# A vision tower on one core: the scan's B product moved from SBUF to PSUM, and each scan step cut into two feature blocks

## The chip, the cores and the metric

The kernel runs on 1 core of a Trainium2 chip. The metric is device time in microseconds (us) of one execution, lower is better; the kernel before is given by the median of three runs.

## What is computed

The reference is a small two-layer vision tower for 32 images, each 38 tokens of 192 features. Cut to what matters here:

```python
h = tokens(x)                                  # patches @ W + b + pos, two class tokens: (32, 38, 192)
h = h + ssm(layernorm(h))                      # first scan
h = h + moe_ffn(layernorm(h))                  # top 2 of 8 experts, 192 -> 768 -> 192, gelu
h = h + mamba_two_ways(layernorm(h))           # down to 96, a forward and a backward scan, up to 192
h = h + mixture(layernorm(h))                  # top 2 of 8 experts, 192 -> 192

# ssm, per token t, feature d and state n (16 states):
state = (delta * state + (1 - delta) * u * b * dt) * exp(a * dt)
y = sum_n(state * c) + u * D
# mamba, once per direction:
h = exp(dt * A) * h + dt * u * B               # B, C: 16 numbers per token
y = sum_n(h * C) + u * D
```

In both layers the recurrence has the form state = decay x state + input x B, per feature and state, along the tokens.

## The kernel before, in words

The images are worked in 4 groups of 8, so a group has T = 304 tokens. Tokens lie along the free dimension, features or states along the 128 partitions. A **scan step** handles QB = 2 feature blocks; a block is 8 features x 16 states = 128 partitions, so one step works on tiles of 128 x 608. 12 steps (QSTEPS) cover the 192 features. What a step does:

- SP fills one of 4 ring slots (SLOTS) by DMA: decay rows into dA and input rows into BB, both broadcast from a scratch tensor rows_d, 304 KB each.
- ACT raises the decay rows to exp (in the first pass this goes into another tile, and POOL multiplies it into dA, `decay_step`, L678).
- DVE multiplies the input rows by the B states, which lie in a PSUM bank: the **B product**, BB <- BB x B, 128 x 608, back into SBUF (`first_b_product` L1243, `b_product` L1273). It is issued one step ahead: step c issues the product of step c+1, then its own scan.
- In the first pass DVE also forms PR = decay x C from PSUM (L1258).
- DVE runs the **scan**, one tensor_tensor_scan of 608 columns from dA and BB, both in SBUF, into ST (`first_step` L1264, `direction_step` L1287).
- POOL multiplies ST by C or PR (L684, L765), and PE sums the 16 states of each feature into the Y bank (all matmuls go through the helper at L1614).

**First pass.** `first_pass` runs three stages side by side, 12 steps each: the scan of group s, the preparation of group p (patches, layer norm, hidden layers of the A, B, C and delta networks in 11 blocks), and the routing of group m. In step 11 PE forms the B states (B1_BANK) and the C states (C1_BANK) of the next group to be scanned: `states(p, 1, ...)` and `states(p, 2, ...)`, and ACT adds a bias to each in PSUM.

**Expert blocks.** 34 blocks of 128 gathered rows, matmul work mostly. Blocks 0 to 4 are put into the last scan steps of the first pass, others stand alone, and the second half goes into the first steps of the second pass.

**Second pass.** For each group `part_a` is 12 steps of the forward scan and `part_b` 12 of the backward scan. Beside the scan of group g, part_a finishes group g-1 (output norm, up-projection, residual) and brings in group g+1; group g-2's expert mixture, begun in the last step of part_b, runs in steps 0 to 4 of part_a as 6 parts on PE (`mixture`). Each part multiplies two expert inputs, gated by POOL (L773), into two banks: features 0 to 127 into Q_BANK and the rest, 64 features, into QR_BANK. In step 5 DVE adds both to the residual (`add_mixture`, Om at L1524, Or at L1525). After the last group the same code runs with nothing beside it.

The order on every engine is written out by hand in these step functions; an engine runs its list in order and waits on semaphores, which count per group. PSUM has 8 banks of 512 columns, and each user has a fixed bank. The layout before (the hidden blocks take banks 5, 6 and the free Y bank in turn):

```python
        Y_BANK = (3, 0)
        MEAN_BANK, ROUTE_BANK = 4, 7
        B1_BANK, C1_BANK = 1, 2
        HIDDEN_BANKS = (5, 6)
        X_BANK, Z_BANK, L_BANK, Q_BANK, QR_BANK = 6, 5, 5, 7, 4
        AFTER_BANK, BW_BANK = Y_BANK, (1, 2)
```

## Time and profile before

| | |
|---|---|
| median of 3 runs | 999.3 us (997.8, 999.3, 1003.47) |
| span of the profiled execution | 1002.8 us; its own run is not marked, and the run nearest to it is the one of 1003.47 us |
| busy over the span | PE 758.7 us (76%), DVE 650.1 (65%), POOL 445.9 (44%), ACT 406.4 (41%) |
| first pass with scans (48 steps) | about 53 to 307 us of the span |
| expert blocks without scans | about 310 to 524 us |
| second pass with scans (96 steps) | about 524 to 928 us |
| last group's end, no scan beside it | about 928 to 1003 us |

How to read it: the span runs from the first to the last instruction of one execution. "Busy" is the time in which an engine executes; the idle time before an instruction is given with the engine and instruction that released it ([0.67 <-ACT ...]). A record's length contains some overlap with the next one, so the spacing of starts is the better price of an instruction in a full queue.

### The profile page before, as it was taken

What the parts mean: (1) busy time and instruction counts of PE and PEld (TensorE: products, weight loads), DVE (VectorE), ACT (ScalarE), POOL (GpSimd) and SP (SyncE); (2) the same over time, 40 slices, a digit from 0 to 9 for tenths busy, and PEclk for the clock granted to TensorE, in tenths of its full rate; (3) what the DMA queues carried; (4) which work ended last, traced back from release to release, by engine and by line L of the source; (5) the groups of instructions that cost most, each with busy time, mean ns of one, the idle gap of its engine ahead of it and who ended that gap; (6) DMA issues with size and microseconds to landing.
All of it is one profiled execution on the core that took longest, in us unless ns stands there. A gap on an engine that the chain in (4) does not pass through costs nothing.

```text
span 1002.8 us, 11291 instructions
## 1 busy us (share of the span) xinstructions
PE 758.7 (76%) x3552; PEld 591.1 (59%) x3552; DVE 650.1 (65%) x993; ACT 406.4 (41%) x880; POOL 445.9 (44%) x311
## 2 busy tenths in 40 slices
PE   7978797775578798889996686768696869766745
PEld 5655565445358697888883455546474646544524
DVE  4187979899965223122127997798788896799320
ACT  2556392571234242324445354626243543442010
POOL 1167656864954113120003644553475427455403
PEclk8979899786769899999996596989697979885957
DMA  9579654553955688888748577756775757586011
GB/s 342 134 254 332 182 157 116 148 129 82 251 164 168 185 248 247 235 258 250 216 148 220 150 193 175 183 154 152 201 183 150 188 143 203 150 196 177 12 28 56
DMA packets 84667, 179.50 MB, mean 179 GB/s; under 512 B 12740, under 2 KB 32832, under 8 KB 83840
## 3 DMA queue, kind: packets, MB, share of 16 engines
q1 hardware_dynamic: 79776, 171.55, 61.5%
q0 software_dynamic: 4832, 7.24, 2.4%
q8 instruction: 28, 0.46, 0.2%
q14 instruction: 31, 0.25, 0.1%
HBM read 158.02 MB, written 20.69 MB: 178 GB/s over the span
## 4 chain that ended last, share of the span: by engine, by line
PE 28%; DVE 19%; issue 7%; DMA 5%; ACT 3%; SPq 3%; POOL 2%; DVEq 0%; POOLq 0%
PE PS L1614 27%; DVE ST L1287 6%; DMA xp<-slots_d 3%; DVE BB L1273 3%; DMA BB<-rows_d 2%; POOL PR L765 2%; DVE p_WV L1343 1%; DVE p_OM L1340 1%; DVE p_TM L1338 1%; ACT L889 1%; DVE q_OM L1340 0%; SPq L536 0%; SPq L549 0%; POOL WX L773 0%; ACT dA L938 0%
## 5 line engine op out<-in xcount | busy, mean ns | idle before, releaser
L1614 PE MATMUL PS<-PR,CM 128*128 128x304 f32 (+1 forms) x672 | 198.3, 440 | 78.7 <-POOL PR L765 64.4
L765 POOL TENSOR_TENSOR PR<-ST,V 128x608 f32<-128x608 f32 x96 | 160.5, 1674 | 190.8 <-DVE ST L1287 166.6
L1614 PEld LDWEIGHTS PS<-PR,CM 128*128 128x128 f32 x672 | 135.2, 235 | 126.8 <-POOL PR L765 82.8
L1287 DVE TENSOR_TENSOR_SCAN ST<-dA,BB 128x608 f32<-128x608 f32 x96 | 162.9, 1701 | 6.4 <-POOL PR L765 5.7
L938 ACT ACTIVATE dA<-dA,negA 128x304 f32<-128x304 f32 x192 | 94.0, 540 | 157.9 <-DMA BB<-rows_d 157.8
L678 POOL TENSOR_TENSOR dA<-dA,aP 128x607 f32<-128x607 f32 x48 | 87.9, 1833 | 55.5 <-ACT aP L958 54.4
L989 ACT ACTIVATE HID<-PS,WX 128x128 f32<-128x128 f32 x204 | 59.2, 367 | 127.1 <-PE PS L1614 126.9
L1475 DVE TENSOR_TENSOR xp<-PS,WXB 128x192 f32<-128x192 f32 x34 | 12.2, 358 | 126.9 <-PE PS L1614 124.5
L1264 DVE TENSOR_TENSOR_SCAN ST<-dA,BB 128x608 f32<-128x608 f32 x48 | 89.5, 1865 | 1.8 <-issue 1.8
L1273 DVE TENSOR_TENSOR BB<-BB,PS 128x608 f32<-128x608 f32 x96 | 74.0, 773 | 25.3 <-DMA BB<-rows_d 24.7
L693 POOL DMA_DIRECT2D outs_d<-xp x34 | 19.0, 558 | 151.5 <-DVE xp L1475 151.4
L1614 PE MATMUL PS<-XT,WX 128*128 128x128 f32 x408 | 82.2, 284 | 0.1
L1614 PE MATMUL PS<-XT,WXR 128*128 128x128 f32 x408 | 81.4, 282 | 0.0
L1614 PE MATMUL PS<-WX,HID 128*128 128x192 f32 x408 | 72.6, 327 | 5.4 <-DVE XT L1468 3.7
L684 POOL TENSOR_TENSOR PR<-PR,ST 128x608 f32<-128x608 f32 x32 | 47.7, 1490 | 57.0 <-DVE ST L1264 50.0
L1614 PEld LDWEIGHTS PS<-WX,HID 128*128 128x128 f32 x408 | 65.8, 190 | 6.3 <-issue 6.3
L1614 PEld LDWEIGHTS PS<-XT,WX 128*128 128x128 f32 x408 | 65.2, 201 | 0.3 <-ACT HID L989 0.3
L1614 PEld LDWEIGHTS PS<-XT,WXR 128*128 128x128 f32 x408 | 64.8, 200 | 0.0
L1614 PE MATMUL PS<-WX,CM 128*128 128x304 f32 x192 | 54.7, 435 | 10.8 <-POOL WX L773 10.8
L1614 PEld LDWEIGHTS PS<-WX,CM 128*128 128x128 f32 x192 | 37.6, 199 | 25.9 <-POOL WX L773 13.1
L773 POOL TENSOR_TENSOR WX<-WX,q_Xm 128x608 f32<-128x608 f32 x16 | 25.7, 1618 | 48.3 <-DMA WX<-gates_d 48.3
L1614 PE MATMUL PS<-HB,CM 96*128 96x152 f32 (+1 forms) x240 | 44.1, 339 | 0.5 <-DVE xp L1475 0.5
(322 smaller groups left out, 1379.4 us busy)
## 6 DMA issues: line engine op xcount, KB each, us to landing
dA<-rows_d SPq DMA_DIRECT2D x144, 304.0 KB, 3.8
BB<-rows_d SPq DMA_DIRECT2D x144, 304.0 KB, 4.5
WX<-ex_m SPq DMA_DIRECT2D x34, 576.0 KB, 4.2
WX<-ex_m SPq DMA_DIRECT2D x34, 387.0 KB, 3.7
slots_d<-WXR SPq DMA_DIRECT2D x8, 960.0 KB, 9.2
WXR<-ex_r SPq DMA_DIRECT2D x34, 192.0 KB, 4.4
WX<-gates_d SPq DMA_DIRECT2D x4, 1216.0 KB, 6.4
CM<-c SPq DMA_DIRECT2D x1, 4430.0 KB, 19.7
```

The source lines that it names most:

```text
L678: nc.gpsimd.tensor_tensor(now[:, 1:], now[:, 1:], before[:, 0:QB * T - 1], ALU.mult).then_inc(ap_ready.sem, 1)
L684: nc.gpsimd.tensor_tensor(PR3[c % 3], PR3[c % 3], STq[:, c % 2], ALU.mult).then_inc(P.product.sem, 1)
L693: pool.dma_start(outs_d[b // HALF_BLOCKS][at:at + 128, :], YB[:, b % 3, :]).then_inc(out_rows[b % 3], 16)
L765: nc.gpsimd.tensor_tensor(PRq[:, c % 2], STq[:, c % 2], DIRS[k].Cw.unsqueeze(1).broadcast_to([128, QB, T]), ALU.mult).then_inc(q_product.s ...
L773: nc.gpsimd.tensor_tensor(GX[:, 2 * part:2 * part + 2, :], GX[:, 2 * part:2 * part + 2, :], x[:, :].unsqueeze(1).broadcast_to([128, 2, T]) ...
L938: last = nc.scalar.activation(dAq[:, slot, i, :], dAq[:, slot, i, :], ACT.Exp, scale=negA[:, j:j + 1])
L989: last = nc.scalar.activation(HX[:, p, f, :], PS[:, wide_bank(b, h), j * 128:(j + 1) * 128], ACT.Gelu, bias=WX[:, p, FFN + f:FFN + f + 1])
L1264: nc.vector.tensor_tensor_scan(flat(STq[:, c % 2], False), flat(dAq[:, slot], False), flat(BBq[:, slot], False), 0.0, ALU.mult, ALU.add).t ...
L1273: nc.vector.tensor_tensor(BBq[:, slot], BBq[:, slot], PS[:, BW_BANK[k], 0:T].unsqueeze(1).broadcast_to([128, QB, T]), ALU.mult).then_inc(b ...
L1287: nc.vector.tensor_tensor_scan(flat(STq[:, c % 2], back), flat(dAq[:, slot], back), flat(BBq[:, slot], back), 0.0, ALU.mult, ALU.add).then ...
L1475: nc.vector.tensor_tensor(YB[:, p, :], PS[:, SHARED_BANK, 256:256 + D], WXB[:, p, :], ALU.add).then_inc(y_copied.sem, 1)
L1614: return nc.tensor.matmul(out, lhsT, rhs, start=first, stop=last)
```

## The change

It does four things.

1. The B product is written to PSUM, to an area of 608 columns (BP[0] in the first pass and for the forward scan, BP[1] for the backward one), as two halves of 304 columns, one for each feature block. The scan is two instructions of 304 columns, each reading dA from SBUF and its half of the product from PSUM.
2. The product is no longer one step ahead. With one product area, step c's first half waits for the first scan half of step c-1 (q_half), its second half for the second (q_scanned). On DVE a step is product 0, product 1, (PR), scan 0, scan 1.
3. PSUM is laid out anew to free those columns. The hidden blocks rotate over two banks, not three; QR_BANK is gone. The rest half of the mixture moves out of `mixture` to the X bank, in a new function `mixture_rest` in steps 5 and 6 of part_a, and its addition (Or) to step 7. The rest of the up-projection goes to the Z bank, that of `back` to the X bank. In the expert blocks 0 to 4 both halves share one bank, so the narrow product of the block before is put between them.
4. In step 11 of the first pass the B states of the next group wait for the end of the running scan, so they are formed after the C states and after the sum of step 10, where they stood first.

```diff
-        Y_BANK = (3, 0)
-        MEAN_BANK, ROUTE_BANK = 4, 7
-        B1_BANK, C1_BANK = 1, 2
+        Y_BANK = (7, 0)
+        MEAN_BANK, ROUTE_BANK = 4, 6
+        B1_BANK, C1_BANK = 2, 1
...
         def hidden_bank(g, i):
-            return (HIDDEN_BANKS + (Y_BANK[g % 2],))[i % 3]
+            return (HIDDEN_BANK, Y_BANK[g % 2])[i % 2]
...
-        X_BANK, Z_BANK, L_BANK, Q_BANK, QR_BANK = 6, 5, 5, 7, 4
+        X_BANK, Z_BANK, L_BANK, Q_BANK = 1, 5, 5, 6
...
+        BW = (PS[:, 2, 0:T], PS[:, 4, BANK - T:BANK])
+        BP = (PSF[:, 4 * BANK - QB * T:4 * BANK], PSF[:, 3 * BANK:3 * BANK + QB * T])
+        BPq = [x.rearrange("p (b t) -> p b t", b=QB) for x in BP]
...
             def first_step(g, c):
 
                 slot = c % SLOTS
-                if c == 0:
-                    first_b_product(g, 0)
-                if c + 1 < QSTEPS:
-                    first_b_product(g, c + 1)
-                if c == 0:
+                if c:
+                    first_b_product(g, c)
+                else:
                     dve.wait_ge(c1_ready.sem, c1_ready.after(g, 1))
...
             def b_product(g, k, c):
...
-                nc.vector.tensor_tensor(BBq[:, slot], BBq[:, slot], PS[:, BW_BANK[k], 0:T].unsqueeze(1).broadcast_to([128, QB, T]),
-                                        ALU.mult).then_inc(b_times_w.sem, 1)
+                for i in range(QB):
+                    done = (q_half, q_scanned)[i if c else 1]
+                    dve.wait_ge(done.sem, done.after(g, k * QSTEPS + c))
+                    nc.vector.tensor_tensor(BPq[k][:, i], BBq[:, slot, i], BW[k], ALU.mult).then_inc(b_times_w.sem, 1)
...
-                nc.vector.tensor_tensor_scan(flat(STq[:, c % 2], back), flat(dAq[:, slot], back),
-                                             flat(BBq[:, slot], back), 0.0, ALU.mult, ALU.add).then_inc(q_scanned.sem, 1)
+                def ordered(ap):
+                    return ap[:, ::-1] if back else ap
+
+                nc.vector.tensor_tensor_scan(ordered(STq[:, c % 2, 0]), ordered(dAq[:, slot, 0]), ordered(BPq[k][:, 0]),
+                                             0.0, ALU.mult, ALU.add).then_inc(q_half.sem, 1)
+                dve.wait_ge(b_times_w.sem, b_times_w.after(g, QB * (n + 1)))
+                nc.vector.tensor_tensor_scan(ordered(STq[:, c % 2, 1]), ordered(dAq[:, slot, 1]), ordered(BPq[k][:, 1]),
+                                             0.0, ALU.mult, ALU.add).then_inc(q_scanned.sem, 1)
...
             def mixture(g, part):
...
                 for i in (2 * part, 2 * part + 1):
-                    name, at = ("ew", i) if i < EXPERTS else ("ewp", i - EXPERTS)
-                    last = into(name, at * D, GX[:, i, :], False, part == MIX_PARTS - 1 and i % 2 == 1)
+                    name, at = ("ew", i * D) if i < EXPERTS else ("ewp", (i - EXPERTS) * D)
+                    last = mm(PS[:, Q_BANK, 0:T], cm(name, at, at + 128), GX[:, i, :], False, part == MIX_PARTS - 1 and i % 2 == 1)
...
+                    if mix is not None and n in (5, 6):
+                        if g is not None:
+                            pe.wait_ge(c_copied.sem, c_copied.after(g, 2))
+                        mixture_rest(mix, n - 5)
```

On DVE, a step of the forward scan in the second pass (steps 1 and 2 of a group; ST and dA are the state and the decay, PS a PSUM bank, a scan is printed as SCALAR_TENSOR_TENSOR). Before:

```order
L1273 TENSOR_TENSOR BB<-BB,PS 128x608 [waits landed2]
L1287 SCALAR_TENSOR_TENSOR ST<-dA,BB 128x608 [waits decay_ready,b_times_w]
L1273 TENSOR_TENSOR BB<-BB,PS 128x608 [waits landed3]
L1287 SCALAR_TENSOR_TENSOR ST<-dA,BB 128x608 [waits q_product,decay_ready,b_times_w]
L1502 TENSOR_TENSOR m_gate<-KEEP,counts 102x24 [waits keep_loaded]
```

and after:

```order
L1291 TENSOR_TENSOR PS<-BB,PS 128x304 [waits q_half,landed1]
L1291 TENSOR_TENSOR PS<-BB,PS 128x304 [waits q_scanned]
L1304 SCALAR_TENSOR_TENSOR ST<-dA,PS 128x304 [waits decay_ready,b_times_w]
L1307 SCALAR_TENSOR_TENSOR ST<-dA,PS 128x304 [waits b_times_w]
L1291 TENSOR_TENSOR PS<-BB,PS 128x304 [waits q_half,landed2]
L1291 TENSOR_TENSOR PS<-BB,PS 128x304 [waits q_scanned]
L1304 SCALAR_TENSOR_TENSOR ST<-dA,PS 128x304 [waits q_product,decay_ready,b_times_w]
L1307 SCALAR_TENSOR_TENSOR ST<-dA,PS 128x304 [waits b_times_w]
L1522 TENSOR_TENSOR m_gate<-KEEP,counts 102x24 [waits keep_loaded]
```

The product of the next step (landed2, landed3 before) no longer stands ahead of a scan, and every instruction of the step now waits for one of DVE's own that stands two places ahead of it.

On PE, step 11 of the first pass between group 0 and group 1 (V and PR rows sum states, p_Hm and p_Hr rows are the token mean, HID rows the B or C states). Before:

```order
L1614 MATMUL PS<-HID,WX 128x304 [waits b_times_w]
L1614 MATMUL PS<-HID,WX 128x304 x2
L1614 MATMUL PS<-p_Hm,ones_d 128x304 [waits p_residual]
L1614 MATMUL PS<-p_Hr,ones_d 128x304
L1614 MATMUL PS<-HID,WX 128x304 [waits c_times_a]
L1614 MATMUL PS<-HID,WX 128x304 x2
L1614 MATMUL PS<-PR,CM 128x152 [waits q_product]
L1614 MATMUL PS<-PR,CM 128x152 x3
```

and after:

```order
L1640 MATMUL PS<-p_Hm,ones_d 128x304 [waits p_residual]
L1640 MATMUL PS<-p_Hr,ones_d 128x304
L1640 MATMUL PS<-HID,WX 128x304 [waits c_times_a]
L1640 MATMUL PS<-HID,WX 128x304 x2
L1640 MATMUL PS<-PR,CM 128x152 [waits q_product]
L1640 MATMUL PS<-PR,CM 128x152 x3
L1640 MATMUL PS<-HID,WX 128x304 [waits q_scanned]
L1640 MATMUL PS<-HID,WX 128x304 x2
```

The B states went from the first place, where they waited for the last B product, to the last, where they wait for the last scan.

On PE, steps 4 to 7 of part_a (WX rows are the mixture, YS rows the up-projection, q_RS the variance of the output norm). Before:

```order
L1614 MATMUL PS<-PR,CM 128x304 [waits q_product]
L1614 MATMUL PS<-PR,CM 128x304
L1614 MATMUL PS<-WX,CM 128x304 [waits x_gated]
L1614 MATMUL PS<-WX,CM 128x304 x3
L1614 MATMUL PS<-q_RS,ones_bn 96x304 [waits bn_squares]
L1614 MATMUL PS<-PR,CM 128x304 [waits q_product]
L1614 MATMUL PS<-PR,CM 128x304
L1614 MATMUL PS<-PR,CM 128x304 [waits q_product]
L1614 MATMUL PS<-PR,CM 128x304
L1614 MATMUL PS<-YS,CM 128x304 [waits y_sum,final]
```

and after:

```order
L1640 MATMUL PS<-WX,CM 128x304 [waits x_gated]
L1640 MATMUL PS<-WX,CM 128x304
L1640 MATMUL PS<-q_RS,ones_bn 96x304 [waits bn_squares]
L1640 MATMUL PS<-PR,CM 128x304 [waits q_product]
L1640 MATMUL PS<-PR,CM 128x304
L1640 MATMUL PS<-q_LW,CM 128x304 [waits c_copied]
L1640 MATMUL PS<-WX,CM 128x304 x6
L1640 MATMUL PS<-PR,CM 128x304 [waits q_product]
L1640 MATMUL PS<-PR,CM 128x304
L1640 MATMUL PS<-WX,CM 128x304 [waits c_copied]
L1640 MATMUL PS<-WX,CM 128x304 x5
L1640 MATMUL PS<-YS,CM 128x304 [waits y_sum,main_mixed]
```

Half of the mixture's instructions moved from the parts in front of the step to two blocks behind the sums of steps 4 and 5 (n = 5 and 6).

## Rows read from the trace of the kernel before

**Rows 1.** Windows by stage: stretch, length, busy time per engine, clock, DMA share, GB/s.

```profile
53.00:107.00 54.00, 41.76 (x153) 29.36 (x152) 47.95 (x52) 32.70 (x56) 40.26 (x23) 0.89 0.91 298
107.00:160.00 53.00, 42.56 (x182) 31.48 (x181) 45.37 (x62) 33.88 (x61) 32.43 (x20) 0.92 0.54 148
330.00:515.00 185.00, 162.59 (x1171) 153.75 (x1170) 40.15 (x150) 70.50 (x200) 33.47 (x45) 0.97 0.77 229
720.00:780.00 60.00, 47.98 (x199) 35.81 (x200) 46.96 (x60) 23.65 (x50) 39.03 (x25) 0.89 0.69 178
```

**Rows 2.** Groups of DVE instructions by line and shape: busy, mean ns, idle before.

```profile
L1287 DVE TENSOR_TENSOR_SCAN ST<-dA,BB 128x608 f32<-128x608 f32 x96 | 162.9, 1701 | 6.4 <-POOL PR L765 5.7 <-DVE BB L1273 0.7
L1264 DVE TENSOR_TENSOR_SCAN ST<-dA,BB 128x608 f32<-128x608 f32 x48 | 89.5, 1865 | 1.8 <-issue 1.8
...
L1243 DVE TENSOR_TENSOR BB<-BB,PS 128x608 f32<-128x608 f32 x48 | 36.9, 774 | 8.8 <-DMA BB<-rows_d 8.4
...
L1371 DVE TENSOR_TENSOR q_Cm<-q_Cm,q_RS 96x304 f32<-96x304 f32 x8 | 3.6, 455 | 1.1 <-ACT q_RS L848 0.8
...
L1149 DVE TENSOR_TENSOR p_Cm<-p_Hm,PS 128x304 f32<-128x304 f32 x8 | 3.6, 451 | 4.4 <-PE PS L1614 4.4
```

**Rows 3.** Line L1273, the B product: ns min/median/max, first and last start.

```profile
L1273 DVE TENSOR_TENSOR BB<-BB,PS x96: 750/773/789, 527.7 to 921.2; 128x608 f32<-128x608 f32 x96
```

**Rows 4.** Timeline of DVE, 665 to 668 us: start, length.

```profile
665.10 1.42 DVE L1287 TENSOR_TENSOR_SCAN ST<-dA,BB 128x608 f32<-128x608 f32 x1
666.44 0.45 DVE L1149 TENSOR_TENSOR q_Cm<-q_Hm,PS 128x304 f32<-128x304 f32 x1
666.80 0.46 DVE L1150 TENSOR_TENSOR q_Cr<-q_Hr,PS 64x304 f32<-64x304 f32 x1
667.18 0.77 DVE L1273 TENSOR_TENSOR BB<-BB,PS 128x608 f32<-128x608 f32 x1
667.88 1.47 DVE L1287 TENSOR_TENSOR_SCAN ST<-dA,BB 128x608 f32<-128x608 f32 x1
```

**Rows 5.** Timeline of all engines, 713.5 to 715 us.

```profile
713.75 1.47 POOL L765 TENSOR_TENSOR PR<-ST,V 128x608 f32<-128x608 f32 x1 [5.58 <-DVE ST L1287]
...
714.27 2.22 DVE L1287 TENSOR_TENSOR_SCAN ST<-dA,BB 128x608 f32<-128x608 f32 x1
```

**Rows 6.** Timeline of all engines, 106 to 110 us, between groups 0 and 1.

```profile
106.03 2.81 PE L1614 MATMUL PS<-HID,WX 128*128 128x304 f32 x6
...
108.68 1.20 PE L1614 MATMUL PS<-PR,CM 128*128 128x152 f32 x8
...
109.40 0.79 DVE L1258 TENSOR_TENSOR PR<-aP,PS 128x608 f32<-128x608 f32 x1 [0.67 <-ACT PS L1036]
```

**Rows 7.** Timelines of PE and DVE, 752 to 765 us, steps 4 to 7 of part_a.

```profile
752.33 2.21 PE L1614 MATMUL PS<-WX,CM 128*128 128x304 f32 x8
...
754.58 0.47 DVE L1524 TENSOR_TENSOR Om<-q_Hm,PS 128x304 f32<-128x304 f32 x1 [4.73 <-PE PS L1614]
...
764.12 2.36 PE L1614 MATMUL PS<-YS,CM 96*128 96x304 f32 x4 [7.02 <-DVE YS L1546]
```

**Rows 8.** Windows of L1287 alone: four stretches of part_a's steps 6 on, 7 scans each.

```profile
sum 87.10, DVE 49.20; mean DVE 12.30
```

**Rows 9.** Windows of L1287 alone: two ends of part_b, 613.5:620.3 and 919.5:926.6, 3 scans each.

```profile
sum 13.90, DVE 11.07; mean DVE 5.53
```

**Rows 10.** Timeline of POOL, the last product of the second pass.

```profile
925.32 2.49 POOL L765 TENSOR_TENSOR PR<-ST,V 128x608 f32<-128x608 f32 x1 [1.36 <-DVE ST L1287]
```

**Rows 11.** Timeline of DVE, the second product of the second pass.

```profile
531.12 0.79 DVE L1273 TENSOR_TENSOR BB<-BB,PS 128x608 f32<-128x608 f32 x1 [2.67 <-DMA BB<-rows_d]
```

**Rows 12.** Timeline of DVE, 163 to 164 us: small instructions, dependent and not.

```profile
163.19 0.17 DVE L1224 TENSOR_TENSOR m_gate<-KEEP,m_gate 102x24 f32<-102x24 f32 x1
163.40 0.18 DVE L1225 TENSOR_REDUCE KEEP<-m_gate 102x3 f32<-102x24 f32 x1
163.49 0.17 DVE L1226 TENSOR_REDUCE KEEP<-m_gate 102x3 f32<-102x24 f32 x1
```

More of the change, by code:

```diff
@@ L388, in vit_tower @@
         block = ctx.enter_context(nc.Block())
-        SHARED_BANK = 3
+        SHARED_BANK = 7
         HALF_FT = FT // 2
@@ L1533, in part_a @@
                         add_mixture(mix)
+                    if mix is not None and n == 7:
+                        add_mixture_rest(mix)
                     if g is not None and n == 6:
@@ L1705, in contract, with by_state @@
                 return mm(out, cm(name + "_r", 0, n), rest, False, True)
-            def by_state(name, s, bank):
-                mm(PS[:, bank, 0:T], cm(name), s.UP[:, 0:T], True, False)
-                return mm(PS[:, bank, 0:T], cm(name + "_r"), s.URrK, False, True)
+            def by_state(name, s, out):
+                mm(out, cm(name), s.UP[:, 0:T], True, False)
+                return mm(out, cm(name + "_r"), s.URrK, False, True)
             def project_states(g, k):
@@ L1797, in patches @@
                     pe.wait_ge(hid_ready.sem, hid_ready.after(p - 1, 11))
+                    pe.wait_ge(delta_ready.sem, delta_ready.after(p - 1, 1))
+                if k and m is not None:
+                    pe.wait_ge(xtok_copied.sem, xtok_copied.after(m, 2))
                 patch_products(p, k)
@@ L1877, in experts @@
                     turn(b + 1)
+                if 0 <= b < SCAN_BLOCKS:
+                    widen(b, (0,))
+                    if b >= 1:
+                        narrow(b - 1)
+                    widen(b, (1,))
+                    return
                 if 0 <= b < BLOCKS:
-                    widen(b)
+                    widen(b, (0, 1))
                 if b >= 1:
@@ L1943, in first @@
                         first_sum(s, n - 1)
+                    if n == 11 and p is not None:
+                        if s is not None:
+                            pe.wait_ge(P.scanned.sem, P.scanned.after(s, QSTEPS))
+                        states(p, 1, B1_BANK).then_inc(b1_mm.sem, 1)
                     if n == 3 and m is not None:
@@ L2016, in part_a @@
                         mixture(mix, n + QSTEPS - MIX_FROM - 1)
+                    if mix is not None and n in (5, 6):
+                        if g is not None:
+                            pe.wait_ge(c_copied.sem, c_copied.after(g, 2))
+                        mixture_rest(mix, n - 5)
                     if nxt == 0 and n in IN_PART_A:
```

132 lines of the change are left out of this document (77 added, 55 removed).

## The prediction

> **What bounds the kernel now.** The page's totals over the whole span fill no engine and name no bound, so I read the busy time by stage [rows 1]. In the first pass from group 1 on (107 to 160 us) DVE has 45.4 of 53 us and PE 42.6: DVE is the bound. At 53 to 107 us DVE is busier still, but the DMA share is 0.91, so both are near their limit. From 330 to 515 us PE has 162.6 of 185 us; no scan runs there, and the change takes nothing from PE. In the second pass (720 to 780 us) PE has 48.0 and DVE 47.0 of 60 us: they take turns at being the bound, and that stage must be read step by step.
>
> On DVE the costliest groups are the scans: 96 x 1701 ns and 48 x 1865 ns [rows 2]. A scan of 608 columns with nothing beside it takes 1.42 us, and the next instruction starts 1.34 us after it (665.10 to 666.44) [rows 4]. The mean is longer because of POOL: at 713.75 us POOL's product starts, the scan at 714.27 begins inside it and takes 2.22 us [rows 5]. The B product, which has one input in SBUF and one in PSUM, never does that: its slowest of 96 is 789 ns, with POOL at work all the while [rows 3].
>
> **The price of a step.** A 304-column product that reads PSUM starts its successor .36 to .38 us later (666.44, 666.80, 667.18); the 608-column product takes .70 (667.18 to 667.88) [rows 4]. So the fixed part is about .06 us, two halves cost .76, and two half scans (1.34 + .06) 1.40. The new scan has the operands of the product (one in SBUF, one in PSUM), so I take it as undisturbed by POOL. In starts, second pass: before .70 + (1.70 - .08) = 2.32 us, after 2.16, 96 x .16 = 15 us of DVE time. First pass: before .70 + (1.865 - .08) = 2.485, after 2.16, 48 x .325 = 15.6 us. That is DVE time; what reaches the end is less.
>
> Reading PSUM may itself cost a fixed part. The rows say no: a 304-column subtraction from PSUM takes 451 ns, a product of two SBUF tiles at the same length 455 [rows 2]. The bounds are -4 ns, and the fixed .06 us doubled, for which no row speaks; I take 0, by the nearest rows. The Trainium skill, "VectorE: DVE Perf Modes", section "The TRN2 errata", gives the fixed part as 58 cycles from SBUF and 120 from PSUM at 0.96 GHz, which speaks against this change. By that page 288 half scans would cost 65 ns more each, 18.7 us; the trace's 451 against 455 ns does not bear it out for two-input instructions.
>
> **First pass, on the path.** Less 15.6 us in DVE time. Of this, group 0 gives 3 back, being near the DMA limit [rows 1]. The changes of group cost most. Before, DVE waited .67 us there, for the C bias [rows 6]: B was long in place. Now the B states follow C (2.81 us) and the sum of step 10 (1.20) on PE [rows 6]. PR, which starts at 109.40, is done .7 us later, and then DVE has nothing ready until B has passed: its three matmuls, as long as C's, run from about 109.8 to 112.6, and the bias follows, so the first product starts near 113.2 instead of 110.1. Of these 3.1 us part would be less where PE is quicker, and some is more where the hidden stage is late; I take 3.4 for each of three changes and 2 for the first group, ahead of which nothing is scanned: 12 us. Two hidden banks instead of three make PE wait for ACT at more of the blocks; this delays the hidden stage, which DVE needs later in the same pass. No row shows it; between 0 and the 1.5 us by which a wait of one block's activation could repeat in each of two groups I take the upper end, 3. Against that, the product comes a step later than before, so of DVE's 8.4 us of waits for landings [rows 2] those outside group 0 go: -3. Sum: -15.6 + 3 + 12 + 3 - 3 = about 0. This stage gives back what it gains. The two halves of expert blocks 0 to 4 on one bank cost 0: they stand in steps that DVE bounds; without this cover each would cost PE a wait for one gelu.
>
> **Second pass, on the path.** Four terms.
>
> - Start: the second product's wait of 2.67 us for its landing stood ahead of the first scan [rows 11]. Now the first scan runs inside that wait: -2.
> - Steps 0 to 5 of part_a for groups 2 and 3 are bound by PE, which runs without a gap until the mixture is done; DVE waits 4.73 us for it [rows 7]. Six parts lose two instructions each, and the bias one: 13 instructions, 26 matmul records at 2.21 / 8 = .28 us [rows 7], 7 us. POOL's gate products must keep up; they also get rid of the contention. I take 6.5 of 7. The rest half runs in steps 5 and 6, where PE idles 7.02 us for YS [rows 7], about 3.6 us at a time: covered. If that cover were gone, 6.5 comes back. Two groups: -13.
> - From step 6 on DVE is the bound. The 28 scans of these four stretches take 49.2 us where 28 x 1.42 would be 39.8 [rows 8]: 9.4 us of contention go, and the halves cost 28 x (2.16 - .70 - 1.34) = 3.4: -6.
> - Ends of part_b: PE's last sum waits for POOL's product, POOL for the scan. Three scans each take 11.07 us where 6 x 1.42 = 8.5 [rows 9], so 2.5 less .7 for the halves, and POOL's product of 2.49 us [rows 10] is 1.47 undisturbed [rows 5], so 1.0 at each of two ends: -4. The other two ends lie under the load of the gates (groups 1 and 2), which DVE's speed does not move.
>
> The backward scans' steps in the middle wait for the router's logits and gates, so their gain is shadowed; 0. At the last group's end main and rest half of the mixture run one behind the other instead of by turns, with the same number of matmuls: 0. Sum: -2 - 13 - 6 - 4 = -25.
>
> So the profiled execution of 1002.8 us would become about 977.5. Its span stands 3.5 us above the median of 999.3; against that median I say **974 us**.
>
> **Rivals.**
>
> *B: half scans with a larger fixed part.* Each of 288 half scans costs .06 us more, the upper bound above: 17 us of DVE time. On the path lie the first pass (96 halves), the four stretches from step 6 on (56) and the two ends (12), 164 of 288 or 57%: 10 us, **984 us**. For it speaks that no row shows a scan from PSUM; against it the 451 and 455 ns [rows 2]. Chance .17. It is the case that the Trainium skill's page on the DVE Perf Modes would give.
>
> *C, slower: DVE's own semaphores.* Every instruction of a step now waits for one of DVE's own. The small instructions show what that costs back to back: .21 us from start to start where the second reads the first (163.19 to 163.40), .09 where not (163.40 to 163.49), so .12 [rows 12]. One instruction of at least .36 us stands between in the new order, which should hide it. If it does not, 4 x 144 x .12 = 69 us, of which 57% is on the path: 39 less 25, **1013 us**. It decides from 25 / (576 x .57) = .076 us per wait on. Against it: the centre and its follower (666.44 to 667.18) show no idle time between instructions with waits, though none is for DVE's own [rows 4]. Chance .14.
>
> *D: no relief from POOL.* The scan still stalls beside POOL when its second input lies in PSUM. Then the second pass keeps 9.4 + 2.5 + 2 = 14 us of contention, and gives -25 + 14 = -11. The first pass keeps 48 x (1.865 - 1.42) = 21 us, of which three groups' worth, 16, is on the path; less the 3 that group 0 would not give back, +13. The sum is +2: **1001 us**. The B product's 789 ns [rows 3] speaks against it, though no scan is shown. Chance .13. The Trainium skill, "SBUF — State Buffer", section "Who interferes with whom", says that only a DVE instruction with two SBUF inputs contends with POOL's reads, so by it D falls.
>
> **How the numbers follow.** The forecast has .56, B .17, C .14, D .13. What a measurement of this kernel can tell from no change is about 0.5%, 5 us: faster is below 994.3, slower above 1004.3. Faster: the forecast and .15 of B, .71. Same: .02 of B and .11 of D, .13. Slower: C and .02 of D, .16. The likeliest case alone spans 960 (DVE gains in the shadowed steps and no cost at the changes of group) to 985 (PE's stretch gives half). For 8 in 10 I take 955 to 1003: it leaves out C and a little at the lower end.
>
> **What would show it.** Half scans: 288, about .77 us each with the longest near the mean; half products 288, about .45. POOL's products come down to near 1.47 us each [rows 5]. DVE busy falls by little, as halves carry overlap in their records. The wait before Om in part_a falls from 4.73 to under 1 us; at the changes of group a wait of 3 us for ACT stands before the first product. Wrong: half scans with a wide spread (D), a narrow spread above .80 (B), or starts within a step further apart than .38 and .70 with no idle time named (C). If the second pass is not shorter by at least 15 us, the PE stretch was not the bound I took it for.

## The result, and the profile after

The changed kernel takes 993.95 us (median of 11 runs, 986.48 to 998.6) against 998.93 us before (11 runs): a ratio of 0.9937, 95% interval 0.9909 to 0.9965. It is faster, by 0.6%. Forecast was 974 us, 2.5% faster. The direction was right and the time lies in the range, but the gain is a fifth of what I said: 5 us, not 25. The profiled execution has a span of 995.8 us. Ratios, here and below, leave out the few executions that ran slower as a whole; medians are of all.

The groups of DVE instructions by line and shape, changed kernel (count | busy us, mean ns | idle before):

```profile
L1291 DVE TENSOR_TENSOR PS<-BB,PS 128x304 f32<-128x304 f32 x192 | 81.3, 468 | 20.2 <-DMA BB<-rows_d 19.4
L1304 DVE TENSOR_TENSOR_SCAN ST<-dA,PS 128x304 f32<-128x304 f32 x96 | 74.8, 779 | 13.2 <-POOL PR L776 6.5 <-ACT dA L949 3.2 <-issue 1.7
L1307 DVE TENSOR_TENSOR_SCAN ST<-dA,PS 128x304 f32<-128x304 f32 x96 | 72.9, 759 | 0.0
L1258 DVE TENSOR_TENSOR PS<-BB,PS 128x304 f32<-128x304 f32 x96 | 40.6, 467 | 7.5 <-ACT PS L1047 7.3
L1278 DVE TENSOR_TENSOR_SCAN ST<-dA,PS 128x304 f32<-128x304 f32 x48 | 37.5, 781 | 2.8 <-issue 2.1 <-POOL dA L689 0.7
L1280 DVE TENSOR_TENSOR_SCAN ST<-dA,PS 128x304 f32<-128x304 f32 x48 | 36.5, 761 | 0.0
```

The line of the first half scan in the second pass (ns min/median/max, first and last start), and POOL's products:

```profile
L1304 DVE TENSOR_TENSOR_SCAN ST<-dA,PS x96: 766/780/787, 537.8 to 923.2; 128x304 f32<-128x304 f32 x96
```

```profile
L776 POOL TENSOR_TENSOR PR<-ST,V 128x608 f32<-128x608 f32 x96 | 142.2, 1481 | 201.6 <-DVE ST L1307 157.7 <-PE PS L1640 43.8
```

These lines answer to [rows 2] and [rows 3]. The step itself came out as priced: half scans of .76 to .78 us, the first ones with a spread of 21 ns, and POOL's products at 1.48 us. From the first half scan to the second .70 us pass (751.12 to 751.82 us in the trace). Of waits for DVE's own instructions inside a step the trace names 8 in front of the 96 first half scans of the second pass, 1.6 us in all. So rivals B, C and D are out by the profile alone: no larger fixed part, next to no uncovered wait for DVE's own instructions, no contention left. DVE's busy time falls by 46 us, 650.1 to 603.6, where the prediction expected little. The gain was made on DVE; little of it arrived at the end.

By the starts of the scans (ns min/median/max, first and last start; the changed kernel's second pass is shown above), before:

```profile
L1264 DVE TENSOR_TENSOR_SCAN ST<-dA,BB x48: 1405/1585/4043, 55.1 to 320.8; 128x608 f32<-128x608 f32 x48
L1287 DVE TENSOR_TENSOR_SCAN ST<-dA,BB x96: 1393/1419/3102, 531.8 to 925.2; 128x608 f32<-128x608 f32 x96
```

Changed kernel, first pass:

```profile
L1278 DVE TENSOR_TENSOR_SCAN ST<-dA,PS x48: 768/781/789, 56.3 to 327.9; 128x304 f32<-128x304 f32 x48
```

From first to last scan the first pass takes 271.6 us, 5.9 more than before (265.7; its last scan starts at 320.8 us, not near 307 as the table ahead of the prediction has it). The second pass takes 385.4 us, 8.0 less, and what follows its last scan 72.6, 5.0 less. The forecast had about 0 for the first pass and -25 for the other two. The prediction named a sign for this: with less than 15 us in the second pass, PE's stretch was not the bound that it was taken for.

Where the gain went shows in DVE's waits in the first pass, 53 to 330 us (waiting instruction, releaser: total us, times, longest). Before:

```profile
DVE BB L1243 <- DMA BB<-rows_d: 8.4, 8, 2.2
DVE m_Xm L1154 <- ACT q_RS L848: 7.6, 2, 4.4
DVE XT L1467 <- PE PS L1824: 5.9, 3, 3.3
DVE PR L1258 <- ACT PS L1036: 2.0, 2, 1.3
```

Changed kernel:

```profile
DVE m_Xm L1165 <- ACT q_RS L859: 16.6, 2, 8.3
DVE XT L1487 <- PE PS L1853: 14.2, 3, 8.9
DVE PS L1258 <- ACT PS L1047: 7.3, 4, 2.6
DVE PR L1270 <- ACT PS L1045: 7.1, 4, 2.6
DVE V L1270 <- PE PS L1640: 4.0, 2, 3.0
DVE PR L1270 <- PE PS L1640: 3.3, 4, 1.2
```

The waits for landings are gone, as said. The two biases (L1045, L1047) cost 14.4 us against 2.0: as waits, the 12 that I gave the changes of group. From the last scan of a group to the first of the next, though, the three changes grew by 7.2 us only (5.1, 5.9 and 4.8 us before, 7.5, 7.2 and 8.3 now), and the first group starts 1.2 later. But the wait for the routing's rstd (q_RS) more than doubled, sums (PR and V behind PE) appear with 7.3 us, and the expert rows (XT) cost 8.3 more.

In the second pass the wait before Om did not fall below 1 us, as I had said it would; it is 4.64 us, although Om comes 4.6 us earlier in the span (749.98 against 754.58 [rows 7]). And a new wait stands at the end of the same part_a. SP's queue there, changed kernel (start, issue time, engine, line, transfer):

```profile
752.61 0.51 SPq L495 DMA_DIRECT2D dA<-rows_d  x1
...
761.40 0.34 SPq L595 DMA_DIRECT2D out_m<-Om  x1
761.78 0.53 SPq L596 DMA_DIRECT2D out_r<-Or  x1
762.36 0.58 SPq L606 DMA_DIRECT2D rows_d<-p_DL  x1
...
765.95 0.59 SPq L495 DMA_DIRECT2D dA<-rows_d  x1
```

And DVE, same stretch:

```profile
749.98 0.47 DVE L1544 TENSOR_TENSOR Om<-q_Hm,PS 128x304 f32<-128x304 f32 x1 [4.64 <-PE PS L1640]
...
756.76 0.63 DVE L1363 TENSOR_TENSOR p_WV<-p_DL,p_UP 128x456 f32<-128x456 f32 x1
...
760.93 0.44 DVE L1549 TENSOR_TENSOR Or<-q_Hr,PS 64x304 f32<-64x304 f32 x1
...
780.76 0.47 DVE L1160 TENSOR_TENSOR p_Cm<-p_Hm,PS 128x304 f32<-128x304 f32 x1 [5.11 <-PE PS L1640]
```

The rows of the next direction are computed at 757.4 us (p_WV), but SP writes them out only at 762.36, 5.0 us later; in the kernel before it does so at 762.66, .2 us after they are computed. Ahead of them in its list stands the store of the output, which waits for Or, and Or moved from step 5 to step 7. All later refills start late, ACT waits for them (7.77 us before its decays at 770.98), the squares stand behind that wait on ACT, and DVE waits 5.11 us for the mean that PE issues behind the squares.

### The profile page after: what moved, and what is told of

Same layout as the page of the kernel before. It is cut to its first block, busy times and chain, and to the rows that moved or that the text cites. A ratio compares the mean times of both kernels' runs of the same rounds, so it can differ in the third digit from the quotient of the medians.

```text
span 995.8 us, 11712 instructions
## 1 busy us (share of the span) xinstructions
PE 750.1 (75%) x3552; PEld 588.7 (59%) x3552; DVE 603.6 (61%) x1281; ACT 407.2 (41%) x880; POOL 396.9 (40%) x311
## 4 chain that ended last, share of the span: by engine, by line
PE 27%; DVE 13%; issue 9%; DMA 7%; ACT 4%; SPq 4%; POOL 2%; DVEq 0%; POOLq 0%
PE PS L1640 26%; DMA BB<-rows_d 3%; DMA xp<-slots_d 2%; DVE PS L1291 2%; DVE ST L1304 2%; POOL PR L776 2%; DVE ST L1307 1%; ACT dA L949 1%; ACT L900 1%; DVE p_OM L1360 0%; POOL WX L784 0%; SPq L547 0%; SPq L495 0%; POOL xp L765 0%; PE PS L1852 0%
## 5 line engine op out<-in xcount | busy, mean ns | idle before, releaser
L1640 PE MATMUL PS<-PR,CM 128*128 128x304 f32 (+1 forms) x672 | 190.7, 430 | 60.0 <-POOL PR L776 49.4
L776 POOL TENSOR_TENSOR PR<-ST,V 128x608 f32<-128x608 f32 x96 | 142.2, 1481 | 201.6 <-DVE ST L1307 157.7
L689 POOL TENSOR_TENSOR dA<-dA,aP 128x607 f32<-128x607 f32 x48 | 71.2, 1483 | 80.3 <-ACT aP L969 75.1
L1291 DVE TENSOR_TENSOR PS<-BB,PS 128x304 f32<-128x304 f32 x192 | 81.3, 468 | 20.2 <-DMA BB<-rows_d 19.4
L1304 DVE TENSOR_TENSOR_SCAN ST<-dA,PS 128x304 f32<-128x304 f32 x96 | 74.8, 779 | 13.2 <-POOL PR L776 6.5
L1307 DVE TENSOR_TENSOR_SCAN ST<-dA,PS 128x304 f32<-128x304 f32 x96 | 72.9, 759 | 0.0
L1640 PE MATMUL PS<-p_Xm,WX 128*128 128x304 f32 x88 | 36.4, 500 | 18.4 <-ACT HID L892 14.3
```

Of the source, the lines that this page charges most:

```text
L689: nc.gpsimd.tensor_tensor(now[:, 1:], now[:, 1:], before[:, 0:QB * T - 1], ALU.mult).then_inc(ap_ready.sem, 1)
L776: nc.gpsimd.tensor_tensor(PRq[:, c % 2], STq[:, c % 2], DIRS[k].Cw.unsqueeze(1).broadcast_to([128, QB, T]), ALU.mult).then_inc(q_product.s ...
L1291: nc.vector.tensor_tensor(BPq[k][:, i], BBq[:, slot, i], BW[k], ALU.mult).then_inc(b_times_w.sem, 1)
L1304: nc.vector.tensor_tensor_scan(ordered(STq[:, c % 2, 0]), ordered(dAq[:, slot, 0]), ordered(BPq[k][:, 0]), 0.0, ALU.mult, ALU.add).then_in ...
L1307: nc.vector.tensor_tensor_scan(ordered(STq[:, c % 2, 1]), ordered(dAq[:, slot, 1]), ordered(BPq[k][:, 1]), 0.0, ALU.mult, ALU.add).then_in ...
L1640: return nc.tensor.matmul(out, lhsT, rhs, start=first, stop=last)
```

## The experiments

Each is the changed kernel with an edit, except the one on the kernel before. Ratios are to the kernel before, run on the same chip; 95% intervals stand behind them. The moves of the up-projection's rest and of `back` to other banks have no run of their own. A difference from the changed kernel is worked out from the two ratios (0.1% is 1 us) and, by their intervals, uncertain by some 4 to 6 us. Together the results read so:

| kernel | median us | ratio | against the changed kernel |
|---|---|---|---|
| changed kernel | 993.95 | 0.9937 (0.9909 to 0.9965) | |
| store behind the refill | 985.4 | 0.9858 (0.9814 to 0.9902) | -8 |
| three hidden banks | 980.5 | 0.9806 (0.9763 to 0.9848) | -13 |
| expert blocks on two banks | 991.97 | 0.9921 (0.9888 to 0.9955) | -2 |
| B states ahead of the sum | 994.08 | 0.9928 (0.9901 to 0.9955) | -1 |
| the four together | 967.15 | 0.9653 (0.9601 to 0.9705) | -28 |
| the first two together | 972.72 | 0.973 (0.969 to 0.977) | -21 |
| product back in SBUF | 1016.44 | 1.0178 (1.0133 to 1.0222) | +24 |
| whole instructions of 608 | 999.94 | 0.999 (0.9955 to 1.0025) | +5 |
| store behind the refill, mixture doubled | 1004.3 | 1.0056 (1.0025 to 1.0087) | +12 |
| kernel before, two hidden banks | 1006.74 | 1.0068 (1.0041 to 1.0095) | |

The starts of the scans in the profiles cut the span into stages (us). Each profile is one execution, whose span lies some 7 us at most from its kernel's median:

| stage | before | changed | store behind the refill | three hidden banks | these two together |
|---|---|---|---|---|---|
| first pass, first to last scan | 265.7 | 271.6 | 267.3 | 257.4 | 255.7 |
| from there to the second pass's first scan | 211.0 | 209.9 | 207.7 | 205.9 | 213.6 |
| second pass, first to last scan | 393.4 | 385.4 | 373.0 | 384.4 | 373.4 |
| from there to the end | 77.6 | 72.6 | 73.7 | 72.8 | 78.0 |

How far a stage varies by itself is seen where the code of a stage is the same: 267.3 to 273.4 us in the first pass (changed, store, mixture doubled), 382.6 to 385.4 in the second (changed, three hidden banks and the two edits behind it), 204.8 to 213.6 between the passes.

**The output store behind the refill.**

```diff
-                    if c == 10 and g >= 2:
-                        store(g - 2)
...
                     read_rows(g, 1, c)
+                    if c == 1 and g >= 2:
+                        store(g - 2)
```

> The changed kernel with one edit: SP's store of a group's output (it waits for the rest half's addition, which the change moved from step 5 to step 7 of part_a) stands behind the second refill of the next direction instead of ahead of the row writes. Theory 1, the moved addition holds SP's queue, and with it the row writes and refills behind it: the row writes of groups 2 and 3 start about 4 us earlier (in the changed kernel 762.4 us, with the rows computed by about 757), the wait of 5.1 us before the centre at the end of part_a (780.8 us) falls below 1.5 us, and the whole is 4 to 8 us shorter than the changed kernel's 994: 986 to 990. Theory 2, the rows land no earlier because the transfers themselves are the limit: the row writes move, the wait of 5.1 us stays above 4, and the whole stays at 992 to 996.

Measured 0.9858, 8 us less than the changed kernel. SP's queue in this kernel, where Om starts at 742.89 us:

```profile
750.49 0.33 SPq L606 DMA_DIRECT2D rows_d<-p_DL  x1
...
753.97 0.55 SPq L495 DMA_DIRECT2D dA<-rows_d  x1
...
763.93 0.59 SPq L595 DMA_DIRECT2D out_m<-Om  x1
```

The row writes start 7.6 us behind Om, in the changed kernel 12.4: 4.8 us earlier, and the wait of 5.11 us before the centre is gone from DVE's list (the only wait named between 730 and 780 us is the one for Om). The second pass's scans:

```profile
L1304 DVE TENSOR_TENSOR_SCAN ST<-dA,PS x96: 768/777/789, 531.5 to 904.5; 128x304 f32<-128x304 f32 x96
```

They take 373.0 us against 385.4. Theory 1 holds, at the strong end of what it said.

**Three hidden banks.**

```diff
-            return (HIDDEN_BANK, Y_BANK[g % 2])[i % 2]
+            return (HIDDEN_BANK, Y_BANK[g % 2], MEAN_BANK)[i % 3]
...
-                    if i >= 2:
-                        pe.wait_ge(hid_ready.sem, hid_ready.after(g, i - 1))
+                    if i >= 3:
+                        pe.wait_ge(hid_ready.sem, hid_ready.after(g, i - 2))
+                    if i == (8 if g else 5):
+                        pe.wait_ge(delta_ready.sem, delta_ready.after(g, 1))
...
-                pe.wait_ge(hid_ready.sem, hid_ready.after(p, 2))
+                pe.wait_ge(hid_ready.sem, hid_ready.after(p, 6 if p else 3))
```

> The changed kernel with three hidden banks in turn again: the bank of the means is free while the hidden blocks run, except for the delta product, and serves as third. Theory 1, the rotation over two banks holds PE and with it the routing's variance and the sums of the scan: DVE's two waits for q_RS (16.6 us) return to about 8, its waits for PE before PR and V (7.3 us) to below 2, and the whole is 8 to 14 us shorter than 994: 980 to 986. Theory 2, these waits come from ACT's order or from the later B states and not from the banks: both sums stay within 2 us of what they were and the whole at 991 to 996.

Measured 0.9806, 13 us less. How two banks hold the routing is seen in the changed kernel, all engines, 131 to 138 us:

```profile
131.60 1.36 PE L1640 MATMUL PS<-p_Xm,WX 128*128 128x304 f32 x2 [2.36 <-ACT HID L892]
...
133.77 1.84 PE L1640 MATMUL PS<-V,CM 128*128 128x304 f32 x4
...
135.44 0.68 PE L1640 MATMUL PS<-q_RS,ones_d 128*128 128x304 f32 x2
...
137.75 1.03 DVE L1165 TENSOR_TENSOR m_Xm<-q_Cm,q_RS 128x304 f32<-128x304 f32 x1 [8.29 <-ACT q_RS L859]
```

The sixth hidden block waits for ACT (2.36 us), ACT is busy with other steps' decays and with table loads (from 126.7 to 131 us in the trace: the decays of a step of the running scan, the routing's squares and two loads), and the sum and the routing's variance (q_RS) are queued behind that block on PE. With three banks these waits of DVE read, in the same window:

```profile
DVE m_Xm L1165 <- ACT q_RS L859: 13.0, 3, 6.1
...
DVE V L1270 <- PE PS L1640: 0.9, 1, 0.9
DVE PR L1270 <- PE PS L1640: 0.8, 1, 0.8
```

The sums' 7.3 us fell to 1.7, as theory 1 says; the wait for q_RS fell only from 16.6 to 13.0, not to 8. A faster scan that comes to it earlier would explain that; no run separates it. The first pass's scans:

```profile
L1278 DVE TENSOR_TENSOR_SCAN ST<-dA,PS x48: 768/779/787, 53.6 to 311.0; 128x304 f32<-128x304 f32 x48
```

They take 257.4 us against 271.6, and 6.2 of these 14 us lie in group 0 (47.6 us from its first to its last scan, now 41.4), beside which no group is routed yet: the waits for sums there fall from 5.3 to .9 us. The time agrees with theory 1.

**Expert blocks 1 to 4 on two banks.**

```diff
-                return ((5, 5) if b < SCAN_BLOCKS else ((5, 3), (1, 2))[b % 2])[h]
+                return ((5, 5) if b == 0 else (5, 4) if b < SCAN_BLOCKS else ((5, 3), (1, 2))[b % 2])[h]
...
```

> The changed kernel with expert blocks 1 to 4 on two banks again (the second is the bank of the means, free there after the token copies). Theory 1, the shared bank holds PE in these blocks and so DVE's copies of the turned rows: the waits for these copies in the last scan group (14.2 us) return to about 6, the second pass starts 5 to 8 us earlier against the first pass's end, the whole 986 to 989. Theory 2, the largest of these waits (8.9 us) comes from the landing of the gathered rows, as PE's own wait of 5.8 us for it says, and the bank costs one activation's wait at a time: at most 3 us less, 991 to 994.

Measured 0.9921, 2 us less, inside the noise; the waits for the copies stay at 14.5 us. Theory 2, as to the bank: sharing it costs nothing that shows beside this uncertainty, and nothing is what I had put down for it.

**The B states ahead of the sum.**

```diff
                         states(p, 2, C1_BANK).then_inc(c1_mm.sem, 1)
+                        if s is not None:
+                            pe.wait_ge(first_half.sem, first_half.after(s, QSTEPS))
+                        states(p, 1, B1_BANK).then_inc(b1_mm.sem, 1)
...
-                            pe.wait_ge(P.scanned.sem, P.scanned.after(s, QSTEPS))
-                        states(p, 1, B1_BANK).then_inc(b1_mm.sem, 1)
```

> The changed kernel with the B states of the next group right behind the C states, ahead of the sum of step 10, and waiting for the first half of the last scan only (their bank is not read by the second half). Theory 1, DVE's wait for the B bias at the three changes of group (2.1, 1.8 and 2.6 us) is PE time on the path: it falls by the sum's 1.2 us and more at each, the whole 3 to 5 us less, 989 to 991. Theory 2, the sum that now comes later holds POOL's and DVE's next products by as much: the wait for the bias falls, a wait for a sum takes its place, 993 to 995.

Measured 0.9928, 1 us less. The wait for B's bias fell from 7.3 to 4.0 us, that for sums (PR and V) grew from 7.3 to 8.6. The time fits theory 2, but that wait is not what took over: from the last scan of a group to the first of the next, the three changes together are 4.8 us shorter (23.0 to 18.2), as theory 1 said. In the profile that gain is lost again in the last group, where PE waits for the first gathered rows of the expert blocks. Changed kernel, then this one:

```profile
285.69 0.47 PE L1852 MATMUL PS<-CM,xp 128*128 128x128 f32 x1 [5.83 <-DMA xp<-slots_d]
```

```profile
285.34 0.48 PE L1852 MATMUL PS<-CM,xp 128*128 128x128 f32 x1 [11.18 <-DMA xp<-slots_d]
```

The group starts 5.7 us earlier (254.3 to 248.6 us) and SP issues the load of these rows 4.7 us earlier (281.23 to 276.53), but it takes 8.8 us until PE starts on them, not 4.5. What held it no run shows, and this is one execution.

**The four together, and the first two.**

> The four edits of the first four experiments together: the output store behind the next direction's second refill, three hidden banks, expert blocks 1 to 4 on two banks, the B states ahead of the sum. Theory 1, the costs of the store (8 us, second pass) and of the hidden banks (13 to 14 us, first pass) lie in different stages and add up: 994 - 8 - 13 - 2 = 971, 967 to 975, a ratio to the kernel before of 0.968 to 0.976. Theory 2, a stage freed of one wait runs into the next (row transfers, ACT), and the sum falls short by half: 980 to 986.

Measured 0.9653, 967 us, the fastest of all versions; the costs add (24 us one by one, 28 together).

> The changed kernel with the two large edits alone, the store behind the refill and three hidden banks, without the edits to the expert blocks and the B states. Theory 1, these two make up nearly all of the gain of the four together (ratio 0.9653): 0.966 to 0.974 of the kernel before, 966 to 974 us. Theory 2, the B states ahead of the sum count once the hidden stage is no longer in the way: 3 to 5 us less than that gain, a ratio of 0.972 to 0.978.

Measured 0.973. Theory 1's ratio, and also within theory 2's: between this and the four together lie 8 us, more than the last two edits gave alone (3 us), with intervals of 0.4 to 0.5% on each. The times do not settle whether they are worth more once the hidden stage is out of the way. The profiles say that the B states are: between these two kernels the three changes of group get 4.7 us shorter (20.84 to 16.18) and the whole first pass 5.0 (255.7 to 250.7), so this time the gain is kept. The rest of the difference lies between the passes (213.6 and 204.8 us), where profiles differ by as much without it.

**The product back in SBUF, all else as changed.**

```diff
-                    nc.vector.tensor_tensor(BPq[0][:, i], BBq[:, slot, i], PS[:, B1_BANK, 0:T], ALU.mult).then_inc(P.b_times_w.sem, 1)
+                    nc.vector.tensor_tensor(BBq[:, slot, i], BBq[:, slot, i], PS[:, B1_BANK, 0:T], ALU.mult).then_inc(P.b_times_w.sem, 1)
...
```

> The changed kernel with its order, halves, waits and PSUM layout, but the product written back into its ring slot in SBUF, so that both inputs of each half scan lie in SBUF as they did before. Theory 1, the PSUM operand is what frees the scan and POOL from each other: half scans spread from .76 to over 1.5 us, POOL's products return to about 1.67 us, and the whole grows by 12 to 30 us, 1006 to 1024. Theory 2, most of that contention lay under other waits: the instructions lengthen as said and the whole stays within 5 us, 990 to 999.

Measured 1.0178, 24 us more than the changed kernel. The first half scan of the second pass:

```profile
L1304 DVE TENSOR_TENSOR_SCAN ST<-dA,BB x96: 772/792/2733, 544.0 to 938.4; 128x304 f32<-128x304 f32 x96
```

Against 766/780/787 with the product in PSUM: the shortest are alike, so reading PSUM costs no fixed part; the longest are 3.5 times as long. Theory 1. One point differs from it: POOL's products with the state stay at 1487 ns here. POOL is not spared, though. Its multiplication into the decay in the first pass, changed kernel and this one:

```profile
L689 POOL TENSOR_TENSOR dA<-dA,aP 128x607 f32<-128x607 f32 x48 | 71.2, 1483 | 80.3 <-ACT aP L969 75.1 <-DMA BB<-rows_d 4.8
```

```profile
L689 POOL TENSOR_TENSOR dA<-dA,aP 128x607 f32<-128x607 f32 x48 | 79.2, 1650 | 70.7 <-ACT aP L969 69.4 <-DMA BB<-rows_d 0.8
```

Over all lines the scans take 70 us more with the product in SBUF (221.7 to 291.8) and POOL's products some 11. With halves the scan pays most of the contention; between the kernel before and whole scans from PSUM (the next experiment) the shares are 48 us and 41. Why they differ stays open.

The Trainium skill, "SBUF — State Buffer", section "Who interferes with whom", says that a DVE instruction with two SBUF inputs contends with a GpSimd instruction that reads SBUF, and that one with at most one SBUF input, outside the two-port modes, does not. These rows agree: 2733 ns at the longest with two, 787 with one. The Trainium skill, "VectorE: DVE Perf Modes", section "The TRN2 errata", has a fixed part of 58 cycles from SBUF and 120 from PSUM; by an estimate from it a PSUM input costs 65 ns more. These rows do not show that: the shortest half scan takes 766 ns with it and 772 without.

**Whole instructions of 608 columns, in PSUM.**

```diff
+                dve.wait_ge(q_scanned.sem, q_scanned.after(g, k * QSTEPS + c))
+                nc.vector.tensor_tensor(BPq[k], BBq[:, slot], BW[k].unsqueeze(1).broadcast_to([128, QB, T]), ALU.mult).then_inc(b_times_w.sem, QB)
...
+                nc.vector.tensor_tensor_scan(flat(STq[:, c % 2], back), flat(dAq[:, slot], back), BP[k][:, ::-1] if back else BP[k],
+                                             0.0, ALU.mult, ALU.add).then_inc(q_scanned.sem, 1)
```

> The changed kernel with one product and one scan of 608 columns per step, both still in PSUM, and so each waiting for the one right ahead of it. Theory 1, a wait for DVE's own last instruction costs about .12 us as it does between small instructions, and the two halves hide it: per step +.24 for two such waits, -.13 for two instructions fewer, +.11 x 144 = 16 us, some 57% of it on the path, 999 to 1006. Theory 2, the wait costs nothing between long instructions and the halves are pure cost: -.13 x 144 = -19 us, on the path about -10, 982 to 988.

Measured 0.999, 999.94 us, 5 us more than the changed kernel, about the size of the uncertainty, at the lower end of theory 1's range; the rows say it more sharply. DVE's timeline:

```profile
677.39 0.78 DVE L1285 TENSOR_TENSOR PS<-BB,PS 128x608 f32<-128x608 f32 x1
678.21 1.42 DVE L1295 TENSOR_TENSOR_SCAN ST<-dA,PS 128x608 f32<-128x608 f32 x1
679.76 0.80 DVE L1285 TENSOR_TENSOR PS<-BB,PS 128x608 f32<-128x608 f32 x1
680.59 1.42 DVE L1295 TENSOR_TENSOR_SCAN ST<-dA,PS 128x608 f32<-128x608 f32 x1
```

Product to scan takes .82 us from start to start, where .70 was free of a wait; scan to product 1.55 against 1.34 [rows 4]. So the price of rival C is real, .12 and .21 us, and the halves in turn hide it. Theory 1.

**The kernel before with two hidden banks.**

```diff
-            return (HIDDEN_BANKS + (Y_BANK[g % 2],))[i % 3]
+            return (HIDDEN_BANKS[0], Y_BANK[g % 2])[i % 2]
...
```

> The kernel before with one edit: the hidden blocks rotate over two banks (5 and the free Y bank) instead of three. Theory 1, the rotation costs the first pass by itself what giving the third bank back to the changed kernel gained: DVE's wait for q_RS grows from 7.6 to about 16 us and the whole by 8 to 14 us, 1008 to 1014. Theory 2, in the kernel before DVE is so full there that the later hidden stage is hidden, and only the faster scan uncovered it: at most 4 us, 999 to 1003.

Measured 1.0068, 7 us more. It lies between the theories. DVE's wait for q_RS, which was 7.6 us:

```profile
DVE m_Xm L1154 <- ACT q_RS L848: 13.2, 2, 7.4
```

So some 7 of the 13 us are the rotation's by itself, and the rest seems to show only once the scan is faster; with 3 to 5 us of uncertainty on each, the shares are rough.

**PE's load in part_a restored.**

```diff
+                    mm(PS[:, Q_BANK, 0:T], cm(name, at, at + 128), GX[:, i, :], False, False)
                     last = mm(PS[:, Q_BANK, 0:T], cm(name, at, at + 128), GX[:, i, :], False, part == MIX_PARTS - 1 and i % 2 == 1)
```

> The kernel of the store experiment with each of the 12 main matmuls of the expert mixture issued twice in its old place, so that PE's load in steps 0 to 4 of part_a is what it was before the rest half moved out (the mixture counts double in the output). Theory 1, PE's instructions alone set the time of the main addition: 24 records at .26 to .28 us put Om 6 to 6.7 us later, from 23.7 us after its group's first scan (groups 2 and 3) to 29.7 or more. Theory 2, PE in the changed kernel waits in that stretch for the gates' landing and for ACT and runs part of it at a lower clock after the wait, so the added work fills these holes: Om comes 1.5 to 4 us later, 25.2 to 27.7 us after the first scan. The whole grows by twice that and some 6 us at the last group's end, where nothing hides it.

Om comes 28.7 and 26.9 us after the first scan of groups 2 and 3 (751.87 - 723.15, 858.71 - 831.80), in the kernel without the doubling 23.7 and 23.6: 5.0 and 3.3 us later. Group 3 fits theory 2, group 2 lies between the two. But the groups differ by the clock. In group 2 both kernels run the 6 us behind PE's wait for the gates at 0.72 of full speed on average; in group 3 the one without the doubling does so (0.72, 820.0 to 826.0 us), the doubled one runs at 1.00 (829.8 to 835.8). Like against like, then, it is 5.0: the 24 records take 6.1 us, and they fill one wait of 1.15 us, of PE for ACT (p_Xm), that the doubled kernel no longer has. The wait for the gates itself stays (3.87 and 3.60 us without the doubling, 3.63 and 3.31 with it). The whole grows by 20 us over the kernel of the store experiment (0.9858 to 1.0056), where 8 from these two groups and some 6 at the end were expected; behind the last scan the profile has 10.5 us more (73.7 to 84.3), as two groups' mixtures are doubled there. What PE filled or waited for in the changed kernel, group 3:

```profile
833.29 1.29 PE L1640 MATMUL PS<-WX,CM 128*128 128x304 f32 x4 [3.57 <-POOL WX L784]
834.42 1.85 PE L1640 MATMUL PS<-HB,CM 96*128 96x304 f32 x6
836.06 2.23 PE L1640 MATMUL PS<-PR,CM 128*128 128x152 f32 x8
```

The same matmuls before (PE, 835 to 838 us):

```profile
835.28 1.19 PE L1614 MATMUL PS<-HB,CM 96*128 96x304 f32 x6
836.31 1.20 PE L1614 MATMUL PS<-PR,CM 128*128 128x152 f32 x8
```

PE now reaches the mixture before the gates have landed and waits 3.57 us (before, .76). Behind that wait matmuls run at the lower clock level, 1.2 GHz (the granted clock from 835 to 838 us is 0.50 of full speed, before 1.00), and the 14 records behind the first four take 4.1 us instead of 2.4. Of the 7 us that I took from PE some 2.8 + 1.7 went there, and 1.15 into the wait for p_Xm. That leaves 1.4, and Om, counted from the group's first scan, comes 1.6 us earlier than before (25.0 to 23.4).

## Why the prediction was wrong in its size

**The price of a step: right.** .76 and 1.40 us, no contention, no fixed part, waits covered. The product in SBUF (+24 us) shows the operand's part; whole instructions (+5, hardly more than the uncertainty) show that of the halves, which the rows price at .12 and .21 us per step.

**First pass, the changes of group: right in kind, too large.** 12 us was said. The two biases cost 14.4 against 2.0, but by the starts of the scans it is 7.2 at the three changes and 1.2 at the start.

**First pass, "two hidden banks instead of three ... 3 us": the first step that failed.** It measured 13 us (0.9806 against 0.9937). I priced one activation's wait in each of two groups. What I did not count is PE's queue: behind a hidden block that waits stand the running scan's sum and the routing's variance, and DVE waits for both. No row of the kernel before shows this, so both ends of the range had to stand; I set the upper end from one activation instead of from the chain that is queued behind it. Group 0 was misread with it: I let it give back 3 us for being near the DMA limit, at 298 GB/s [rows 1]. With three hidden banks it runs in 41.4 us against 49.9 before, at 348 GB/s (53.6 to 95.0 us).

**Second pass, the moved rest half "covered": the second step that failed.** The matmuls are covered: YS, ready at 758.9 us, starts on PE at 759.0 in the changed kernel. But the step that was moved issues more than matmuls: its addition moved two steps on DVE, SP's store waits for that addition, and SP's list has the next direction's row writes and refills behind it. I named no queue behind Or. It measured 8 us (12 in the second pass by the starts of the scans, less elsewhere).

**Second pass, the terms.** With the store put right, the scan starts tell what the terms gave (kernel with the store behind the refill against the kernel before): steps 0 to 5 of groups 2 and 3, -4 us for -13 forecast (53.6 to 49.6); from step 6 on, -5.6 for -6 (four stretches, 106.2 to 100.6); the backward directions up to the last group's step 6, -10.6 for -2, and from there to the end -5.1 for -2; the start +0.3 for -2; group 1's first steps +0.7. Sum -24 for -25. The sum held by luck: PE's stretch was mis-sized by 9 us, since a shorter load for PE ran into the landing of the gates, a lower clock and a wait for ACT, and the backward steps, which I had put down as shadowed by the router, gave that back.

At the last group's end I had said 0. In the profiles the mean there reads, before and changed (PE):

```profile
954.10 1.38 PE L1614 MATMUL PS<-q_Hm,ones_d 128*128 128x304 f32 x2 [1.06 <-DVE q_Hr L1550]
```

```profile
949.27 0.78 PE L1640 MATMUL PS<-q_Hm,ones_d 128*128 128x304 f32 x2 [1.13 <-DVE q_Hr L1576]
```

The rest half's 24 records now run where PE had idled 2.73 us before the up-projection, and the matmuls behind it run at the higher clock level, 2.4 GHz (granted clock from 940 to 952 us 1.00; before, from 952 to 966, 0.50). I saw the same number of matmuls, not the gap that they would fill. This gain is not steady, however: with the store behind the refill and three hidden banks the gap is filled as well, and the end takes 78.0 us, no less than before (77.6). There PE waits 2.41 us for the gates (changed kernel 1.58), and the granted clock behind that wait is 0.86 (906 to 918 us; changed kernel, 929 to 941 us, 1.00).

So the forecast's sum of 25 comes out for the change without its two side effects: 994 less 8 and less 10 (13 measured, 3 counted) is 976, where 974 was said, and the run of the two edits together gave 972.7. Its parts do not come out. In that run's profile the first pass is 10 us shorter than before, where the forecast without the banks has some 3, and the second pass with the end 20, where it has 25.

## What to carry to other kernels

When a buffer or a bank is taken from one stage to serve another, price the whole queue behind the instruction that will wait for it, on every engine that issues in order, and not the wait by itself. When an instruction is moved, follow its last semaphore to each queue that waits for it: here an output store, of no hurry to anyone, held the loads of the next direction for 5 us. A faster engine finds such holds first: with both undone the same change is worth 2.7%, not 0.6%.

## What the runs showed of the hardware

Two things I had not expected. A DVE instruction that waits for the one right ahead of it costs .12 us behind a 608-column product and .21 behind a 608-column scan; one 304-column instruction between hides all of it. And contention with POOL is not shared evenly: in 608-column form the scan of the second pass took up to 3.1 us and POOL's product 1674 ns on average; in halves with both inputs in SBUF the scan took up to 2.73 us for half the work and POOL's product with the state stayed at 1487, though its product with the decay took 1650 against 1483.
